# Second and third bf16 pieces made two steps behind the first, in place of one

## The reference

```
h = patches(x) @ W + b + pos_emb
h = h + attention(layernorm(h))              # 12 heads
h = h + slot_moe(layernorm(h))               # soft slots: 4 experts x 256 slots, hidden 768
h = h + low_rank_attention(layernorm(h))     # 6 heads, rotary, causal
h = h + routed_moe(layernorm(h))             # 32 experts, 4 used per token, hidden 768

# slot_moe, per image b (n: token, e: expert, s: slot)
logits   = einsum('bnd,esd->bnes', x, phi)
dispatch = softmax(logits, axis=n);  combine = softmax(logits, axis=(e, s))
slots    = einsum('bnd,bnes->besd', x, dispatch)
hid      = gelu(einsum('besd,edh->besh', slots, w1) + b1)
out      = einsum('besd,bnes->bnd', hid @ w2 + b2, combine)
```

## Time and profile before

| | us |
|---|---|
| median of 3 runs | 1087.37 (1079.14 to 1090.16) |
| the profiled execution | 1087.47 |
| its span, first to last instruction | 1085.7 |
| this stage, its first PE instruction to the next stage's first | 91.55 |

### The profile page before, as it was taken

The page is one execution under the profiler, slowest core; times in us unless marked ns, Lnnn a source line. Parts: engine busy times, 40 slices in busy tenths (PEclk is TensorE's granted clock), DMA queues, the critical chain, the costliest instruction groups (busy, mean ns, idle before and its releaser), DMA issues. The chain is left out here.

```text
span 1085.7 us, 20284 instructions
## 1 busy us (share of the span) xinstructions
PE 980.4 (90%) x7536; PEld 647.1 (60%) x7536; DVE 384.1 (35%) x1041; ACT 666.3 (61%) x1226; POOL 297.6 (27%) x354
## 2 busy tenths in 40 slices
PE   8888859779999999999999999884279999999997
PEld 8455535433444444444444446653169999999996
DVE  2554858561111112221212122376722222222233
ACT  0474948579988888888888885482123444333332
POOL 0111753231133310000000000000565655555531
PEclk9888979899999999999999999597579999999999
DMA  9000018989655655555555530106479999999984
GB/s 359 17 2 1 2 57 316 320 331 183 134 122 112 131 121 120 122 118 117 117 117 117 117 88 2 30 1 173 174 247 326 323 327 326 332 324 325 317 252 129
DMA packets 76350, 185.90 MB, mean 171 GB/s; under 512 B 15784, under 2 KB 34632, under 8 KB 75992
## 3 DMA queue, kind: packets, MB, share of 16 engines
q1 hardware_dynamic: 64012, 169.95, 52.4%
q0 software_dynamic: 11808, 14.39, 6.4%
q10 hardware_dynamic: 432, 0.26, 0.1%
HBM read 148.87 MB, written 35.69 MB: 170 GB/s over the span
## 5 line engine op out<-in xcount | busy, mean ns | idle before, releaser
L1238 ACT ACTIVATE sle_H<-sle_hp 128x1024 f32<-128x1024 f32 x384 | 367.3, 1024 | 53.4 <-PE sle_hp L1160 53.4
L1726 ACT ACTIVATE ext_H<-ext_hp,ext_bias 128x128 f32<-128x128 f32 x378 | 104.1, 398 | 162.1 <-issue 159.0
L1177 PE MATMUL sle_up<-sle_H,sle_cw 128*32 128x512 f32 (+1 forms) x2048 | 191.4, 492 | 0.0
L1668 PE MATMUL ext_yp<-rmoe_w,ext_H 128*128 128x192 f32 x756 | 133.5, 326 | 1.1 <-issue 0.6
L1270 DVE STREAM_TRANSPOSE sle_UT<-sle_up 128x256 f32<-128x256 f32 x64 | 37.3, 583 | 264.3 <-PE sle_up L1177 264.3
L1824 POOL DMA_INDIRECT sum<-ext_y,ext_yi x61 | 97.1, 1592 | 94.8 <-DVE ext_gate L1748 49.9
L1668 PEld LDWEIGHTS ext_yp<-rmoe_w,ext_H 128*128 128x128 f32 x756 | 121.5, 190 | 1.5 <-issue 1.5
L1140 POOL COPY sle_cw<-keep_CT 128x128 f32<-128x128 f32 x64 | 18.8, 295 | 354.1 <-PE sle_up L1177 354.0
L1160 PE MATMUL sle_hp<-keep_G,keep_dT 99*128 99x512 bf16 (+1 forms) x512 | 101.9, 332 | 7.9 <-PEq L927 6.8
L1177 PEld LDWEIGHTS sle_up<-sle_H,sle_cw 128*32 128x32 f32 x2048 | 53.5, 109 | 87.0 <-issue 73.4
L1160 PE MATMUL sle_hp<-sle_G,sle_dT 99*128 99x512 bf16 (+1 forms) x512 | 99.9, 327 | 1.1 <-ACT sle_H L1238 1.1
(11 more groups left out here) (278 smaller groups left out, 1195.2 us busy)
## 6 DMA issues: line engine op xcount, KB each, us to landing
rmoe_w<-W SPq DMA_DIRECT2D x126, 576.0 KB, 5.8
pieces<-hid_gp SPq DMA_DIRECT2D x16, 1152.0 KB, 4.9
keep_G<-pieces SPq DMA_DIRECT2D x32, 288.0 KB, 4.1
sle_G<-pieces SPq DMA_DIRECT2D x32, 288.0 KB, 4.0
pieces<-hid_gp SPq DMA_DIRECT2D x8, 768.0 KB, 5.7
keep_G<-pieces SPq DMA_DIRECT2D x32, 192.0 KB, 4.1
sle_G<-pieces SPq DMA_DIRECT2D x32, 192.0 KB, 4.0
keep_CT<-xT SPq DMA_DIRECT2D x6, 512.0 KB, 6.5
```

The lines of the kernel that those rows point to most:

```text
L1177: mm = pe.matmul(to[32 * e:32 * e + 32], cw[:, p, 2 * e + grp, :], H[:, p, h:h + width], start=(p == 0 and grp == 0), stop=(p == 1 and grp ...
L1238: act.activation(H[:, p, WIDTH * k:WIDTH * (k + 1)], hp[k % DEEP][:].rearrange("p a c -> p (a c)"), ACT.Gelu_apprx_tanh).then_inc(gelu_don ...
L1668: mm = pe.matmul(yp[:, 0:D], H[:, q, c, :], rt.w2[:, w, c, :], start=(c == 0), stop=(c == HC - 1))
L1726: act.activation(H[:, q, c, :], hp[q][:, c % 2, (c // 2) * P:(c // 2 + 1) * P], ACT.Gelu, bias=bias[:, q, c:c + 1]).then_inc(gelu_done, 1)
```

## The change

ACT's second piece and the DVE's third piece (and with the second, POOL's third piece) move from one step behind to two steps behind the copy; two of each are left over for the end in place of one.

```diff
@@ block.scalar
-                if n >= 1:
-                    second(n - 1)
+                if n >= 2:
+                    second(n - 2)
+            second(len(steps) - 2)
             second(len(steps) - 1)
@@ block.vector
-                if n >= 1 and steps[n - 1][1] not in ON_POOL:
-                    third(n - 1)
+                if n >= 2 and steps[n - 2][1] not in ON_POOL:
+                    third(n - 2)
+            for n in (len(steps) - 2, len(steps) - 1):
+                if steps[n][1] not in ON_POOL:
+                    third(n)
```

## The result

The changed kernel takes 1090.36 us in the median of 20 runs (1082.75 to 1096.28), the kernel before 1087.29 in 20 runs beside it (1078.76 to 1091.32): ratio 1.0081, 95% interval 1.0053 to 1.0108, so it is slower by some 0.8% (8.8 us). The medians are only 3.1 us apart; they are of all runs, and the ratio is of the fast ones alone. The profiled execution spans 1092.4 us against 1085.7.

A forecast was written before the change was run, and what follows sets the result against it. The prediction took the PE to bound the stage, with a store-and-buffer loop close behind. Loop 2.9, last-tile wait 0 to 0.4 and tail 0.5 made 3.4 to 3.8, middle 3.6, over 1087.47: 1091.1 us, range 1083 to 1098.

The forecast's parts named there:

- The PE sets the pace, so no gain: Undisturbed tiles: PE busy 9.37 of 9.37 us and never waiting for second or third pieces, so no gain.
- The stores come later and make a loop: Later last stores make ACT wait for piece buffers: loop 9.80 us a tile against the PE's 9.37, costing 2.9 us.
- the stall: ACT's 7.50 us store wait at tile 5's first copy; predicted to end 2.9 later and swallow tiles 3 and 4's losses.
- The PE's wait in the last tile: 0 to 0.4: Tile 7: its first copy waits for tile 5's last store, so the PE waits 0 to 0.4 us for a rest.
- The tail: +0.5: After the last copy: three second pieces remain instead of two, and POOL's last third piece starts 0.5 us later.
- The DVE's new wait: hidden: Rests wait for buffers freed by third pieces, some on POOL; one microsecond of cover hides it from the PE.
- the rival of the falling clock: Tiles 3 to 7: short PE waits drop the clock, 2.3 us a fall, 11.5 in five tiles; 1102.5 us, chance 0.05.
- Hidden: Rival: the store loop stays below 9.4 us and only the tail is left, +0.5, 1088.0 us; chance 0.18.
- Transfers queued: Rival: every tile's last store takes 6.4 us to land, the loop 11.5 a tile; 1096.4 us, chance 0.12.

The follow-up runs named there:

- after_both: Changed kernel with a semaphore for each part of a piece buffer and the next stage's loads issued after tile 5's stores; stage 85.21 us, ratio 0.9978.
- both: Kernel before the change with a semaphore per buffer part and the next stage's loads issued after tile 5's stores; stage 84.57 us, ratio 0.9925.
- after_parts: Changed kernel with a semaphore per buffer part, so a copy waits only for its own part's store; stage 92.77 us, ratio 1.0008.
- store_late: Kernel before the change, but each tile's last store also waits for the next tile's first third piece; stage 94.13 us, ratio 1.0127.
- after_late: Changed kernel with the next stage's loads issued after tile 5's stores instead of tile 2's; stage 91.35 us, ratio 1.0046.
- before_parts: Kernel before the change with a semaphore per buffer part; stages 84.90 and 85.20 us in two runs, ratios 0.9874 and 0.9898.
- after_tail: Changed kernel with the last tile put back to one step behind on ACT and the DVE; stage 95.93 us, ratio 1.0130.
- dve_only: Changed kernel with ACT's second pieces back at one step behind, only the DVE two behind; ratio 1.0097, in a rerun (dve_only_again) 1.0010 with stage 99.36 us.

## Why the prediction was right, and where it was short

The forecast was 1091.1 us, 3.6 over before; the medians differ by 3.1, the stages by 7.2. So the direction and the first part are right, and the stage's loss is half missed. That the median of 1090.36 lies so near the forecast is luck: the stage lost twice what I forecast, and the ratio, 1.0053 to 1.0108 or 5.8 to 11.7 us, fits the 7.2 and not the 3.6.

*The PE sets the pace, so no gain.* Right: tile 2 is 9.37 of 9.37, and with all store waits removed the changed order runs at the same pace as the old one (after_both, both).

*The stores come later and make a loop.* Right in mechanism and size: second piece 4 behind copy 6, tile 0's store at 19.30 from the stage's start (predicted 19.1), loop 9.73 (9.80), tile 5 later by 2.72 (2.9). after_parts, which takes only the wait away, and store_late, which adds only the later store, show that this is the cause for tiles 2 to 4. Tile 5's shift does not need the loop for all of it: in after_parts, without a loop, tile 5 is still 1.8 to 2.1 later than in before_parts, by the later store alone. after_late shows that the stall covered what tiles 3 and 4 lost. Tile 6 started at 222.35, where I had it at 222.2, but with no wait for stores: ACT was busy until then.

*The PE's wait in the last tile: 0 to 0.4.* Somewhat small. Tile 7's first copy came 2.20 late against tile 5's. The landing was 6.1 (228.27 + 6.1 = 234.37, copy at 234.49), within the ends I had; but tile 5's last store left 5.92 after tile 6's first copy (222.35) and not 5.00, because in that tile ACT still waited 0.83 for the PE before the next copy. On the PE that became 0.7, and 0.4 more went after the restart at the low clock; together 1.1: the last pair's first copy started at 239.28, which is 88.02 from the stage's start against 84.18, +3.84, of which 2.72 is the stall's shift.

*The tail: +0.5.* **This is the step that failed.** I followed ACT's and POOL's last pieces and left the DVE out. From the last pair's first copy to the last store it took 9.21 us (239.28 to 248.49) in place of 5.90 (235.07 to 240.97), 3.31 more and not 0.5. The rests of the last steps queue behind third pieces; one rest waits for its buffer until POOL is done, and one third piece is held up by another on POOL. With the sizes measured the sum is 2.7 + 1.1 + 3.3 = 7.1 in place of 2.9 + 0.2 + 0.5. after_tail, which puts back the order of the last tile alone, wins 2.1 of it after tile 7's first copy.

*The DVE's new wait: hidden.* Right for the tiles at full pace: rests waited for POOL, 8.0 us in nine waits over the stage, and tiles 1 and 2 still took 9.37. Wrong as a price: I had allowed for the buffer only, not for two third pieces standing in each other's way, and dve_only shows that this alone can make the DVE the bound. In the changed kernel it stayed small by the accident of who comes first: four of POOL's third pieces were stretched and two of the DVE's. In after_parts the order turned behind the stall, and the DVE's were stretched four times.

*Rivals.* The clock stayed at 1.00 in tiles 4, 5 (up to the stall) and 7 with one PE wait of 0.44 to 0.61 us in each, so the rival of the falling clock has nothing for it here. The rule of the Trainium skill that stood beside it (TensorE: Matmul & The Clock Gate, A second HAM failure mode: psum-queue depth-cycling) is not borne out for waits of this size. Hidden is out (tile 2 waits). Transfers queued in part: the last stores of tiles 0, 1 and 4 took 4.7 us, those of tiles 2 and 5 took 6.0 and 6.1, and not each 6.4.

Open: the 0.45 us ahead of the rest of step 38 (242.08), which ends no wait that the trace shows; and how much of the 7.6 to 7.9 us that the new order costs under a semaphore per part is due to the DVE's third pieces beside POOL's.

## What to carry to other kernels

Before deepening a software pipeline, follow the oldest value to where its buffer is freed: with two buffers, one step more made tile 0's last store 2.2 us later (19.30 against 17.08 from the stage's start), and only 1.1 us of that was slack. Then price the drain at the end for each engine's queue, not for the ones that issue last. A wait on a whole buffer can be a wait on its last part: here three semaphores in place of one took 6.3 to 6.6 us from the stage, without any change of order. And measure the stage behind as well: moving the loads took up to 7.6 us from this stage and gave 7.5 to 9.4 to the next.

## What the runs showed of the hardware that I had not expected

A DVE subtraction with both inputs in SBUF and a POOL subtraction, also from SBUF, did not run at once in these traces. If POOL starts first, the DVE's (128x768) ends 0.81 to 0.82 us after POOL's end, however early it began (15 of 15 pairs in dve_only_again); if the DVE starts first, POOL's is the one stretched, to 2.27 us from 1.65 in the changed kernel, and ends 1.50 after the DVE's. The DVE's rests, one of whose inputs is in PSUM, took 0.94 to 0.96 us (1.21 to 1.23 for the wide ones) beside POOL as without it. In the kernel before the third pieces began only 0.04 to 0.19 us before POOL's ended, and the slowest of that size took 1.00 us in place of 0.95, so next to nothing of it could be seen there.

The Trainium skill has the rule (SBUF — State Buffer, Who interferes with whom): a DVE instruction with two SBUF inputs contends with a GpSimd one that reads SBUF, over shared ports that it calls an exclusive lock, and the issue order decides who blocks. The durations above agree; which port is shared no run here can show. The prediction lacks a rival that follows from it, the DVE's third pieces beside POOL's; in dve_only it came true.
